# Expert rows weighed on ScalarE and summed on GpSimd, instead of both in one operation on VectorE

## The chip, the core and the metric

The kernel runs on one core of a Trainium2 chip. The metric is the device time of one execution in microseconds (us); lower is better. A core has five engines with a queue of instructions each: TensorE (PE, matrix products), VectorE (DVE), ScalarE (ACT), GpSimd (POOL) and SyncE (SP, which here only issues DMAs). Each runs its own queue in program order, and engines wait for each other on semaphores.

## The reference

One layer: `out = x + attention(xn) + experts(xn)`, with `xn` the layer norm of `x`. x has 16 x 512 rows of 128 floats.

```python
x = L0_attn_query
xn = _layernorm(x, axis=-1)
x = x + _L0_attn_ref(xn, ...) + _L0_ffn_ref(xn, Wg, W1, b1, W2, b2)
...
# _L0_ffn_ref: 8 experts, the two best of each row count
scores = x_flat @ Wg
topk_scores, topk_idx = jax.lax.top_k(scores, K)
topk_w = jax.nn.softmax(topk_scores, axis=-1)
cw = (jax.nn.one_hot(topk_idx, E, dtype=x.dtype) * topk_w[..., None]).sum(axis=1)
for e in range(E):
    h = jax.nn.gelu(x_flat @ W1[e] + b1[e], approximate=False)
    out_e = h @ W2[e] + b2[e]
    y = y + cw[:, e:e + 1] * out_e
```

The attention is over the 8 heads of each row, not over rows: per row complex states are built, turned by a few gates, multiplied head by head (the "pattern"), put through a softmax for four circuits and used to weigh the values (the "weighted" products). For the change it matters only that it fills the engines around the expert sum.

## The kernel before

The 8192 rows are 16 blocks of 512 (128 partitions x T = 4 x 128 floats). The program is a hand-written order: steps k = -1 to 16, and in each step every engine has its list of calls for block k, for the block before (o = k - 1) and for the one after (n = k + 1). Step 8 spans about 826 to 911 us of the profiled execution, step 9 to 1002, step 10 to 1103, step 14 about 1362 to 1438; step 16 is only the end.

**Experts.** Four blocks are a group. `route` and `row_numbers` (VectorE) find for each row its two experts, the gates and the places in a table that is sorted by expert; GpSimd scatters the rows of xn there (32 indirect DMAs a group, L1294), in the steps 2, 6 and 10 and the step behind each, as well as at the start for the first group. The table is worked off in 39 tiles a group, some ten tiles a step (TensorE `tile_up`, `tile_down`; ScalarE `gelu`, `copy_turn`). When a group is done, GpSimd gathers both results of each row back (`gather`, 8 indirect DMAs a block, into a tile of `got`; for the last two blocks into two unused buffers of xnT), and `combine` adds them to `yacc`, the output block that already holds x and the attention's part. Its step and place are set by `combined_at`: blocks 0, 4 and 8 in the middle of steps 4, 8 and 12; 1 and 2 in step 5, 5 and 6 in step 9, 9 and 10 in step 13, of which the first in the middle and the second at the end; 3, 7 and 11 in the middle of steps 6, 10 and 14; 12 in the middle and 13 and 14 at the end of step 15; 15 in step 16. SyncE stores a block at the start of the step after.

**What stands around it.** VectorE in the middle of a step: `pattern_power` (ends with `below`), `combine`, `turned_states` (L1720), `probabilities` (expo), `value_phase`, `grown_twice` (fxyT, L1705), then the weighted products w0 and w1 (L1665), the sum of w4 (L1689), and so on. ScalarE there: `turn`, `score_exp`, the squares of `control2` (L1036, L1037), `pass_last` (a DMA from its queue, after turned_states), one tile with gelu, the square root `amplitude` (L1085), on which all weighted products wait. GpSimd makes the products pattern 2 and 5 (L1268, 128x1024 each half) and w4, w5, w6 (L1276, four parts each) in one slot of `prod`, so each waits for VectorE's sum of the one before; and the sums of squares sqx (L1259), for which TensorE waits with `grow_once` and `grow_twice` (L786).

**End of a step.** VectorE: product w7, `combine` of the second block, sum of w7; then step k + 1: the product pattern 0, `route` if it is a routed step (2, 6, 10), the sum of w6, more sums, pattern 1, `row_numbers`, `clip_and_mix` (L1760). ScalarE: `abs_sign` (L1103, L1105), then `copy_sums` (L1072) in a routed step, `copy_tile` of kq (L1057), `copy_v`, gelu. The product w4 is `products(k, ("weighted", 4))` in the code, its sum `sums(k, ("weighted", 4))`.

Of the kernel before, what the change touches and what calls it, by code (L numbers as in the profile page):

```python
# [128 lines left out]
def build(nc, query, W_qkv, b_qkv, W_out, b_out, quantum_weights, photonic_phases, entanglement_gates,  # L129
# [28 lines left out]
    with ExitStack() as ctx:  # L158
# [256 lines left out]
        added_step = signal("added_step", 2 * T)  # L415
# [15 lines left out]
        def exists(k):  # L431
            return 0 <= k < NB
# [512 lines left out]
        def _(act):  # L945
# [191 lines left out]

            def copy_mT(k):
                act.wait_ge(mT_psum.sem, mT_psum.value(k))
                if k >= 1:  # L1140
                    act.wait_ge(o_psum.sem, o_psum.value(k - 1))
                act.activation(measT[:], ps_t[:], ACT.Copy).then_inc(mT_ready.sem, 1)
# [17 lines left out]
            for k in STEPS:  # L1160
# [42 lines left out]
                if exists(n):  # L1203
                    pass_last(n)
                tiles(k, 5, 6)
# [18 lines left out]
                if exists(k):  # L1224
                    abs_sign(k, 2)

        @block.gpsimd
        def _(pool):
# [84 lines left out]

            def scatter_part(k, part):
# [9 lines left out]
            for k in STEPS:  # L1324
# [15 lines left out]
                if exists(k):  # L1340
                    products(k, ("weighted", 4))
                    products(k, ("weighted", 5))
# [4 lines left out]
                for b in gathered_at.get(k, [])[3:]:  # L1347
                    gather(b)

        @block.vector  # L1350
        def _(dve):
# [425 lines left out]
            def combine(k):  # L1777
                g, at = k // GROUP, combine_order.index(k)
                dve.wait_ge(got_landed.of(at), got_landed.value(at))
                dve.wait_ge(gates_step.sem, gates_step.value(g))  # L1780
                dve.wait_ge(attn_added.sem, attn_added.value(k))
                for choice in range(2):
                    for t in range(T):
                        if choice == 1:
                            dve.wait_ge(added_step.sem, added_step.value(at, t + 1))
                        tile = k % GROUP * T + t
                        dve.scalar_tensor_tensor(yacc[:, k % YS, t, :], got_at(at)[:, choice, t, :],
                                                 gates[:, g % GS, choice, tile:tile + 1], yacc[:, k % YS, t, :],
                                                 ALU.mult, ALU.add).then_inc(added_step.sem, 1)

# [8 lines left out]
            for k in STEPS:  # L1799
# [49 lines left out]
                for b in combined_at.get(k, [])[0:1]:  # L1849
                    combine(b)  # L1850
# [28 lines left out]
                for b in combined_at.get(k, [])[1:]:  # L1879
                    combine(b)  # L1880
# [27 lines left out]
```

## Time and profile before

| | |
|---|---|
| time of three runs | 1533.66 us median (1532.86 to 1537.47) |
| the profiled execution's own time | 1530.29 us |
| its span, first to last instruction | 1528.3 us |
| instructions | 19285 |
| mean granted TensorE clock | 0.873 of full speed |
| HBM read, written | 113.95 MB, 32.14 MB |

The profile shows one execution: when each engine was busy, with which line, and what ended each wait. The chain that ended last is followed back from the last instruction, at each step to what released it; only what stands on it sets the time. Most of it is a braid of all engines that repeats in each step (about 85 us a step).

### The profile page before, as it was taken

The numbers are of one execution on the slowest core, as the hardware profiler recorded it, in microseconds if no ns is written. First come the engines' busy times: TensorE is split into PE (matmuls) and PEld (weight loads), VectorE is DVE, ScalarE is ACT, GpSimd is POOL, SyncE is SP. The second block draws the span as 40 slices with busy tenths as digits, with TensorE's granted clock in tenths as the row PEclk, the third lists the DMA queues.
The fourth block names the chain that finished last, engine by engine and source line by source line (L and its number), as shares of the span: only waits on it lengthen the run. The fifth ranks groups of instructions, "written<-read, shape, count | busy, mean of one in ns | idle before, by whom it ended". The sixth has DMA issues, their size and how long they took to land.

```text
span 1528.3 us, 19285 instructions
## 1 busy us (share of the span) xinstructions
PE 1109.9 (73%) x5921; PEld 849.3 (56%) x5921; DVE 1269.2 (83%) x1546; ACT 792.0 (52%) x1610; POOL 765.0 (50%) x596
## 2 busy tenths in 40 slices
PE   4355696869788796866969696883977878586834
PEld 2324474747566574745747474672755657374623
DVE  4653899898997997879978979797789898799976
ACT  3424475664647474554646556373545657365321
POOL 2073424365645355375455444657614544554673
PEclk9987897989999898878979798897989989798866
DMA  7333242332415152331524233152331516242111
GB/s 213 97 100 93 54 135 59 117 105 67 145 48 170 39 156 70 107 118 53 152 66 130 76 108 103 51 166 64 111 87 56 146 38 180 56 123 79 40 41 35
DMA packets 111558, 147.37 MB, mean 96 GB/s; under 512 B 15777, under 2 KB 85089, under 8 KB 110945
## 3 DMA queue, kind: packets, MB, share of 16 engines
q1 hardware_dynamic: 102240, 125.15, 27.3%
q0 software_dynamic: 8192, 16.79, 3.4%
q10 hardware_dynamic: 1024, 4.20, 2.1%
q8 instruction: 49, 0.80, 0.2%
q14 instruction: 53, 0.43, 0.1%
HBM read 113.95 MB, written 32.14 MB: 96 GB/s over the span
## 4 chain that ended last, share of the span: by engine, by line
PE 48%; issue 13%; DVE 12%; POOL 12%; ACT 11%; DMA 1%; SPq 1%; ACTq 0%; DVEq 0%; POOLq 0%
PE ps_r L786 8%; PE ps_t L739 7%; PE ps_h L660 7%; PE ps_q L739 5%; PE ps_f L668 5%; PE ps_t L746 4%; POOL sqx L1259 3%; PE ps_k L726 3%; POOL rows_in L1294 3%; POOL prod L1268 3%; POOL got L1309 2%; DVE pat L1689 2%; ACT hid L1122 2%; POOL prod L1276 2%; DVE xy L1481 1%
## 5 line engine op out<-in xcount | busy, mean ns | idle before, releaser
L786 PE MATMUL ps_r<-sqx,mats 128*128 128x512 f32 x256 | 182.9, 853 | 199.5 <-POOL sqx L1259 181.1
L1276 POOL TENSOR_TENSOR prod<-expo,vT 128x512 f32<-128x512 f32 x192 | 236.9, 1266 | 137.6 <-DVE u L1689 97.7
L1268 POOL TENSOR_TENSOR prod<-kq 128x1024 f32<-128x1024 f32 x64 | 149.9, 2364 | 283.1 <-ACT kq L1057 283.0
L1122 ACT ACTIVATE hid<-ps_h,w_tile 128x128 f32<-128x128 f32 x624 | 178.5, 371 | 138.0 <-PE ps_h L660 132.1
L1689 DVE TENSOR_REDUCE pat<-prod 128x128 f32<-128x2048 f32 x96 | 217.1, 2275 | 0.6
L660 PEld LDWEIGHTS ps_h<-turned,w_tile 128*128 128x128 f32 x1248 | 172.5, 207 | 78.0 <-issue 54.2
L660 PE MATMUL ps_h<-turned,w_tile 128*128 128x128 f32 x1248 | 180.9, 292 | 37.8 <-issue 18.8
L786 PEld LDWEIGHTS ps_r<-sqx,mats 128*128 128x128 f32 x256 | 59.4, 257 | 267.3 <-POOL sqx L1259 187.2
L1259 POOL TENSOR_TENSOR sqx<-sqx,sqy 128x512 f32<-128x512 f32 x64 | 87.0, 1380 | 226.3 <-ACT sqy L1037 160.6
L1665 DVE TENSOR_TENSOR prod<-expo,ps_v 128x2048 f32<-128x2048 f32 x80 | 180.8, 2279 | 8.9 <-PE ps_t L739 5.9
L1660 DVE TENSOR_TENSOR prod<-ps_q,kq 128x1024 f32<-128x1024 f32 x128 | 150.3, 1215 | 36.4 <-PE ps_q L842 19.1
L1689 DVE TENSOR_REDUCE u<-prod 128x256 f32<-128x2048 f32 x64 | 145.9, 2281 | 39.0 <-POOL prod L1276 38.5
L668 PE MATMUL ps_f<-w_tile,hid 128*128 128x128 f32 x1248 | 170.9, 282 | 0.5 <-ACT turned L1115 0.5
L1294 POOL DMA_INDIRECT rows_in<-xn,row_of x128 | 138.4, 1081 | 49.1 <-issue 35.4
L668 PEld LDWEIGHTS ps_f<-w_tile,hid 128*128 128x128 f32 x1248 | 158.2, 199 | 0.8 <-ACT hid L1122 0.6
L1309 POOL DMA_INDIRECT got<-rows_out,row_of x112 | 128.6, 1148 | 32.2 <-issue 29.9
L739 PE MATMUL ps_q<-prod,ident 128*128 128x256 f32 x512 | 118.0, 390 | 19.5 <-DVE prod L1665 19.5
L739 PE MATMUL ps_t<-prod,ident 128*128 128x256 f32 x512 | 125.7, 402 | 6.1 <-DVE prod L1665 3.2
L739 PEld LDWEIGHTS ps_q<-prod,ident 128*128 128x128 f32 x512 | 100.7, 197 | 41.8 <-DVE prod L1665 22.2
L739 PEld LDWEIGHTS ps_t<-prod,ident 128*128 128x128 f32 x512 | 101.1, 203 | 21.7 <-issue 3.8
L1103 ACT ACTIVATE u_sgn<-ps_q,tiny 128x512 f32<-128x512 f32 x16 | 11.0, 687 | 181.7 <-PE ps_q L739 181.7
L746 PE MATMUL ps_t<-u,sup_mats 128*128 128x512 f32 x128 | 65.6, 659 | 20.4 <-DVE u L1481 20.3
(265 smaller groups left out, 2075.0 us busy)
## 6 DMA issues: line engine op xcount, KB each, us to landing
w_tile<-w_cat SPq DMA_DIRECT2D x156, 514.0 KB
x_tile<-rows_in SPq DMA_DIRECT2D x156, 64.0 KB
rows_out<-turned SPq DMA_DIRECT2D x156, 64.0 KB
rows_in<-u SPq DMA_DIRECT2D x2, 2496.0 KB, 11.9
yacc<-in_L_attn_query_dram SPq DMA_DIRECT2D x16, 256.0 KB, 4.3
out_dram<-yacc SPq DMA_DIRECT2D x16, 256.0 KB, 3.2
x_sb<-in_L_attn_query_dram SPq DMA_DIRECT2D x11, 256.0 KB, 4.3
b_tile<-b_parts SPq DMA_DIRECT2D x156, 0.8 KB
```

Source lines behind the costliest of these rows:

```text
L660: last = nc.tensor.matmul(ps_h[:, c, :], w_tile[:, n % WS, c * P:(c + 1) * P], turned[:, x_turn(n) % FS, 0, :], start=True, stop=True)
L668: nc.tensor.matmul(ps_f[:, 1, :], hid[:, n % 2, c, :], w_tile[:, n % WS, HID + c * C:HID + (c + 1) * C], start=(c == 0), stop=False)
L739: last = nc.tensor.matmul(ps_u[part][:, ABS_PARTS[part].index(unit[1]), :], ident[:], prod[:, slot, j * 256:(j + 1) * 256], start=(j == 0) ...
L786: nc.tensor.matmul(ps_r[:, bank, :], m, sqx[:, g, :], start=True, stop=True).then_inc(sig.sem, 1)
L1122: act.activation(hid[:, n % 2, c, :], ps_h[:, c, :], ACT.Gelu, bias=w_tile[:, n % WS, HID + HC * C + c:HID + HC * C + c + 1]).then_inc(hid ...
L1268: last = pool.tensor_tensor(set_of(2, part), q, other, ALU.mult)
L1276: last = pool.tensor_tensor(dst[:, at], w[:, at], v[:, at], ALU.mult)
L1294: pool.indirect_dma_start(out=rows_in[g % GI], out_offset=bass.IndirectOffsetOnAxis(ap=row_of[:, g % GS, choice, t:t + 1], axis=0), in_=xn ...
L1309: pool.indirect_dma_start(out=got_at(at)[:, choice, t, :], out_offset=None, in_=rows_out[g % GS], in_offset=bass.IndirectOffsetOnAxis(ap=r ...
L1660: last = dve.tensor_tensor(set_of(slot, part), q, other, ALU.mult)
L1665: last = dve.tensor_tensor(weighted_slot(slot, unit[1]), w, v, ALU.mult)
L1689: dve.tensor_reduce(dst, src, AX_X, ALU.add).then_inc(summed.sem, 1)
```

## The change

`combine` (16 blocks, on VectorE, eight operations `yacc = got * gate + yacc` of 128x128 each) goes. In its place ScalarE has `weigh_rows`: eight copies a block in place, `got = got * gate`, one for each choice and row tile. GpSimd has `add_rows`: two sums a block of 128x512, `yacc = yacc + got[choice]`. ScalarE's place is behind `pass_last` for the first block of a step and at the step's very end for the others; GpSimd's is between the products w4 and w5 for the first and at the step's end for the others. GpSimd waits for half a block (four copies) before each sum, and for its own first sum before the second.

```diff
--- before.py
+++ after.py
@@ -412,7 +412,8 @@
         turn_copied = signal("turn_copied")
         hidden_psum = signal("hidden_psum")
         hidden_ready = signal("hidden_ready", HC)
-        added_step = signal("added_step", 2 * T)
+        added_step = signal("added_step", 2)
+        rows_weighed = signal("rows_weighed", 2 * T)
 
         block = ctx.enter_context(nc.Block())
 
@@ -1135,6 +1136,16 @@
                         gelu(n + 1)
                     copy_turn(y_turn(n), slice(0 if s + 2 < TILES else 1, 2))
 
+            def weigh_rows(k):
+                g, at = k // GROUP, combine_order.index(k)
+                act.wait_ge(got_landed.of(at), got_landed.value(at))
+                act.wait_ge(gates_step.sem, gates_step.value(g))
+                for choice in range(2):
+                    for t in range(T):
+                        tile = k % GROUP * T + t
+                        act.activation(got_at(at)[:, choice, t, :], got_at(at)[:, choice, t, :], ACT.Copy,
+                                       scale=gates[:, g % GS, choice, tile:tile + 1]).then_inc(rows_weighed.sem, 1)
+
             def copy_mT(k):
                 act.wait_ge(mT_psum.sem, mT_psum.value(k))
                 if k >= 1:
@@ -1202,6 +1213,8 @@
                     control2(n)
                 if exists(n):
                     pass_last(n)
+                for b in combined_at.get(k, [])[0:1]:
+                    weigh_rows(b)
                 tiles(k, 5, 6)
                 if exists(k):
                     amplitude(k)
@@ -1223,6 +1236,8 @@
                 tiles(k, 9, None)
                 if exists(k):
                     abs_sign(k, 2)
+                for b in combined_at.get(k, [])[1:]:
+                    weigh_rows(b)
 
         @block.gpsimd
         def _(pool):
@@ -1311,6 +1326,15 @@
                             in_offset=bass.IndirectOffsetOnAxis(ap=row_of[:, g % GS, choice, k % GROUP * T + t:k % GROUP * T + t + 1],
                                                                 axis=0)).then_inc(got_landed.of(at), 16)
 
+            def add_rows(k):
+                at = combine_order.index(k)
+                pool.wait_ge(attn_added.sem, attn_added.value(k))
+                for choice in range(2):
+                    pool.wait_ge(rows_weighed.sem, rows_weighed.value(at, (choice + 1) * T))
+                    if choice == 1:
+                        pool.wait_ge(added_step.sem, added_step.value(at, 1))
+                    tt(yacc[:, k % YS], yacc[:, k % YS], got_at(at)[:, choice], ALU.add, added_step)
+
             def scatter_part(k, part):
 
                 for g, at in ((routed_group(k), part), (routed_group(k - 1) if k >= 0 else None, 4 + part)):
@@ -1339,6 +1363,9 @@
                     gather(b)
                 if exists(k):
                     products(k, ("weighted", 4))
+                for b in combined_at.get(k, [])[0:1]:
+                    add_rows(b)
+                if exists(k):
                     products(k, ("weighted", 5))
                 scatter_part(k, 2)
                 scatter_part(k, 3)
@@ -1346,6 +1373,8 @@
                     products(k, ("weighted", 6))
                 for b in gathered_at.get(k, [])[3:]:
                     gather(b)
+                for b in combined_at.get(k, [])[1:]:
+                    add_rows(b)
 
         @block.vector
         def _(dve):
@@ -1774,20 +1803,6 @@
                 dve.wait_ge(base_loaded.of(k), base_loaded.value(k))
                 tt(yacc[:, k % YS], ps_t[:].rearrange("p (t c) -> p t c", t=T), yacc[:, k % YS], ALU.add, attn_added)
 
-            def combine(k):
-                g, at = k // GROUP, combine_order.index(k)
-                dve.wait_ge(got_landed.of(at), got_landed.value(at))
-                dve.wait_ge(gates_step.sem, gates_step.value(g))
-                dve.wait_ge(attn_added.sem, attn_added.value(k))
-                for choice in range(2):
-                    for t in range(T):
-                        if choice == 1:
-                            dve.wait_ge(added_step.sem, added_step.value(at, t + 1))
-                        tile = k % GROUP * T + t
-                        dve.scalar_tensor_tensor(yacc[:, k % YS, t, :], got_at(at)[:, choice, t, :],
-                                                 gates[:, g % GS, choice, tile:tile + 1], yacc[:, k % YS, t, :],
-                                                 ALU.mult, ALU.add).then_inc(added_step.sem, 1)
-
             first_norms()
             angle_constants()
             normalise(0)
@@ -1846,8 +1861,6 @@
                     grown_once(n, 1)
                 if exists(k):
                     pattern_power(k)
-                for b in combined_at.get(k, [])[0:1]:
-                    combine(b)
                 if exists(n):
                     turned_states(n)
                 if routed is not None:
@@ -1876,8 +1889,6 @@
                     sums(k, ("weighted", 5))
                 if exists(k):
                     products(k, ("weighted", 7))
-                for b in combined_at.get(k, [])[1:]:
-                    combine(b)
                 if exists(k):
                     sums(k, ("weighted", 7))
```

ScalarE, the end of step 9 and the start of step 10 (routed). Before (u_sgn and u are `abs_sign`, tile_sums is `copy_sums`, kq `copy_tile`, hid `gelu`):

```order
L1122 ACTIVATE hid<-ps_h,w_tile 128x128 x4
L1115 ACTIVATE turned<-ps_f 128x256
L1103 ACTIVATE u_sgn<-u,tiny 128x512
L1105 ACTIVATE u<-u 128x512
L1072 ACTIVATE tile_sums<-ps_t 128x128
L1057 ACTIVATE kq<-ps_k 128x512
L1063 ACTIVATE ps_v<-vT 128x512
L1122 ACTIVATE hid<-ps_h,w_tile 128x128 x4
L1115 ACTIVATE turned<-ps_f 128x256
L1103 ACTIVATE u_sgn<-u,tiny 128x512
```

And in the changed kernel:

```order
L1123 ACTIVATE hid<-ps_h,w_tile 128x128 x4
L1116 ACTIVATE turned<-ps_f 128x256
L1104 ACTIVATE u_sgn<-u,tiny 128x512
L1106 ACTIVATE u<-u 128x512
L1146 ACTIVATE got<-got,gates 128x128 x8
L1073 ACTIVATE tile_sums<-ps_t 128x128
L1058 ACTIVATE kq<-ps_k 128x512
L1064 ACTIVATE ps_v<-vT 128x512
L1123 ACTIVATE hid<-ps_h,w_tile 128x128 x4
L1116 ACTIVATE turned<-ps_f 128x256
```

Eight copies in place (got, by gates) now stand between `abs_sign` and `copy_sums`; what follows is as before.

GpSimd, from the second part of step 9 (gathers of block 6, then w4, w5, w6 as prod<-expo,vT) to the first products of step 10 (prod<-kq is a pattern product, rows_in the scatter). Before:

```order
L1309 DMA got<-rows_out,row_of 128x128 x8
L1276 TENSOR_TENSOR prod<-expo,vT 128x512 x12
L1268 TENSOR_TENSOR prod<-kq 128x1024 x2
L1294 DMA rows_in<-xn,row_of 4992x128 x10
L1309 DMA got<-rows_out,row_of 128x128 x8
L1268 TENSOR_TENSOR prod<-kq 128x1024 x2
L1259 TENSOR_TENSOR sqx<-sqx,sqy 128x512 x2
```

And in the changed kernel:

```order
L1324 DMA got<-rows_out,row_of 128x128 x8
L1291 TENSOR_TENSOR prod<-expo,vT 128x512 x4
L1274 TENSOR_TENSOR yacc<-yacc,got 128x512 x2
L1291 TENSOR_TENSOR prod<-expo,vT 128x512 x8
L1274 TENSOR_TENSOR yacc<-yacc,got 128x512 x2
L1283 TENSOR_TENSOR prod<-kq 128x1024 x2
L1309 DMA rows_in<-xn,row_of 4992x128 x10
L1324 DMA got<-rows_out,row_of 128x128 x8
L1283 TENSOR_TENSOR prod<-kq 128x1024 x2
L1274 TENSOR_TENSOR sqx<-sqx,sqy 128x512 x2
```

The twelve parts of w4 to w6 are now cut after the first four by the two sums of block 5, and the two sums of block 6 stand ahead of the pattern product and the scatters.

ScalarE, the last instructions of the program (steps 15 and 16; measT is `copy_mT`). Before:

```order
L1103 ACTIVATE u_sgn<-ps_t,tiny 128x512
L1105 ACTIVATE u<-ps_t 128x512
L1103 ACTIVATE u_sgn<-u,tiny 128x512
L1105 ACTIVATE u<-u 128x512
L1103 ACTIVATE u_sgn<-u,tiny 128x512
L1105 ACTIVATE u<-u 128x512
L1142 ACTIVATE measT<-ps_t 128x512
```

And in the changed kernel:

```order
L1104 ACTIVATE u_sgn<-ps_t,tiny 128x512
L1106 ACTIVATE u<-ps_t 128x512
L1104 ACTIVATE u_sgn<-u,tiny 128x512
L1106 ACTIVATE u<-u 128x512
L1146 ACTIVATE got<-got,gates 128x128 x8
L1146 ACTIVATE xnT<-xnT,gates 128x128 x8
L1104 ACTIVATE u_sgn<-u,tiny 128x512
L1106 ACTIVATE u<-u 128x512
L1153 ACTIVATE measT<-ps_t 128x512
L1146 ACTIVATE xnT<-xnT,gates 128x128 x8
```

Sixteen copies (blocks 13 and 14) now stand ahead of the last sign and absolute value, and eight (block 15) behind measT.

## Rows read from the trace of the kernel before

**Rows 1.** The page's first part: busy us (share of the span) xinstructions.

```profile
PE 1109.9 (73%) x5921; PEld 849.3 (56%) x5921; DVE 1269.2 (83%) x1546; ACT 792.0 (52%) x1610; POOL 765.0 (50%) x596
```

**Rows 2.** Groups of VectorE: line, operation, shapes, count | busy us, mean ns | idle before.

```profile
L1787 DVE SCALAR_TENSOR_TENSOR yacc<-got,gates,yacc 128x128 f32<-128x128 f32 x112 | 34.9, 381 | 0.0
```

**Rows 3.** The chain in order of time: start us, us, what.

```profile
691.97 1.23 DVE yacc L1787 x5
...
1052.92 1.23 DVE yacc L1787 x5
```

**Rows 4.** Timeline of ScalarE, step 8: start us, us, instructions [idle before <-releaser].

```profile
851.79 1.25 ACT L991 ACTIVATE xn<-x_sb,moments,rstd 128x128 f32<-128x128 f32 x3
...
866.88 1.04 ACT L1037 ACTIVATE sqy<-xy 128x1024 f32<-128x1024 f32 x1
...
868.96 1.28 ACT L1122 ACT_TABLE_LOAD   x1 [1.03 <-DVE fxyT L1720]
870.25 1.14 ACT L1122 ACTIVATE hid<-ps_h,w_tile 128x128 f32<-128x128 f32 x4
...
872.98 1.15 ACT L1085 ACTIVATE expo<-expo,eps_amp 128x1024 f32<-128x1024 f32 x1
```

**Rows 5.** GpSimd's sums of squares: ns min/median/max, first and last start.

```profile
L1259 POOL TENSOR_TENSOR sqx<-sqx,sqy x64: 1253/1265/2251, 75.1 to 1405.8; 128x512 f32<-128x512 f32 x64
```

**Rows 6.** Timelines of VectorE, TensorE and GpSimd, middle of step 8.

```profile
874.48 4.47 DVE L1665 TENSOR_TENSOR prod<-expo,ps_v 128x2048 f32<-128x2048 f32 x2
...
877.87 7.07 PE L739 MATMUL ps_q<-prod,ident 128*128 128x256 f32 x32
...
881.60 4.94 POOL L1276 TENSOR_TENSOR prod<-expo,vT 128x512 f32<-128x512 f32 x4 [2.40 <-DVE u L1689]
```

**Rows 7.** Timelines of ScalarE and TensorE, middle of step 6.

```profile
702.33 1.15 ACT L1085 ACTIVATE expo<-expo,eps_amp 128x1024 f32<-128x1024 f32 x1 [1.14 <-DVE expo L1481]
...
706.30 2.53 PE L786 MATMUL ps_r<-sqx,mats 128*128 128x512 f32 x4 [3.07 <-DVE fxyT L1705]
```

**Rows 8.** Timelines of ScalarE, VectorE and GpSimd, start of step 10.

```profile
1001.68 0.26 ACT L1072 ACTIVATE tile_sums<-ps_t 128x128 f32<-128x128 f32 x1
...
1004.91 2.34 DVE L1660 TENSOR_TENSOR prod<-ps_q,kq 128x1024 f32<-128x1024 f32 x2
1007.36 0.17 DVE L1629 TENSOR_SCALAR scan<-scan 128x8 f32<-128x8 f32 x1
...
1002.57 4.67 POOL L1268 TENSOR_TENSOR prod<-kq 128x1024 f32<-128x1024 f32 x2 [14.41 <-ACT kq L1057]
1011.60 1.76 POOL L1294 DMA_INDIRECT rows_in<-xn,row_of  x1 [4.36 <-DVE tile_expert L1649]
```

**Rows 9.** Timelines of VectorE and GpSimd, start of step 6.

```profile
644.70 1.45 DVE L1535 TENSOR_SCALAR ss<-ss 128x96 f32<-128x96 f32 x1
...
643.73 4.68 POOL L1268 TENSOR_TENSOR prod<-kq 128x1024 f32<-128x1024 f32 x2 [17.14 <-ACT kq L1057]
```

**Rows 10.** Timelines of VectorE and ScalarE, end of step 13 and start of 14.

```profile
1347.35 4.12 DVE L1787 SCALAR_TENSOR_TENSOR yacc<-got,gates,yacc 128x128 f32<-128x128 f32 x8
...
1362.41 2.36 DVE L1660 TENSOR_TENSOR prod<-ps_q,kq 128x1024 f32<-128x1024 f32 x2
...
1361.70 0.58 ACT L1057 ACTIVATE kq<-ps_k 128x512 f32<-128x512 f32 x1
```

**Rows 11.** Timelines of VectorE and ScalarE, end of step 15 and step 16.

```profile
1498.95 3.16 DVE L1787 SCALAR_TENSOR_TENSOR yacc<-got,gates,yacc 128x128 f32<-128x128 f32 x8
1502.04 2.17 DVE L1787 SCALAR_TENSOR_TENSOR yacc<-xnT,gates,yacc 128x128 f32<-128x128 f32 x8
...
1523.29 2.19 DVE L1787 SCALAR_TENSOR_TENSOR yacc<-xnT,gates,yacc 128x128 f32<-128x128 f32 x8
...
1502.20 0.63 ACT L1105 ACTIVATE u<-u 128x512 f32<-128x512 f32 x1
1508.63 0.72 ACT L1103 ACTIVATE u_sgn<-u,tiny 128x512 f32<-128x512 f32 x1 [5.80 <-DVE u L1689]
...
1520.22 0.60 ACT L1142 ACTIVATE measT<-ps_t 128x512 f32<-128x512 f32 x1 [10.21 <-PE ps_t L754]
```

## The prediction

> **What bounds the kernel now.** The page's first part comes first: VectorE is busy 83% of the span and TensorE 73% [rows 1]. No engine is full, so moving work off the fullest one is worth only what the chain that ended last holds of it. The groups of VectorE give the size of what goes: 112 of the 128 operations of `combine` cost 34.9 us [rows 2], 16 more about 5.5 by a like length. Reported lengths overlap, though: eight of them pass in 2.2 us. Then I asked the chain where `combine` stands on it. It does in the middle of steps 6 and 10 [rows 3] and at the end of the program; in the other steps the chain runs past it, through TensorE, GpSimd or ScalarE. So of some 35 us of VectorE time about 11 are on the path: twice 2.1, then 5.1 and 2.2 [rows 11].
>
> **The costs of the new work.** No row shows a 128x128 ScalarE copy from SBUF with a scale per partition. The nearest from below is gelu with one pointer operand, four in 1.14 us, so one each 0.26 us and eight in 2.2; from above the layer norm with two pointers, three in 1.25 us, so one each 0.39 and eight in 3.2 [rows 4]. Copy has one pointer, but reads SBUF; I take 0.29 each, 2.35 for a block. It needs no table load (`copy_tile` and the squares stand beside others without one). A GpSimd sum of 128x512 stands in the trace: 1.25 us at least, 1.27 in the middle, 2.25 at worst [rows 5]; two are 2.55 us. The Trainium skill ("GPSIMD Engine Reference", section 3.1) states that a two-input fp32 operation is about half as fast there as on VectorE. An estimate from its 4497 ns for 2048 elements is 1.12 us for 512, so 2.25 for two; by it the end would cost 0.3 us less than below. The trace has the same form at 1.27, and the sum uses that row.
>
> **Steps 4, 8 and 12, middle: 0.** The place is ahead of gelu and of the square root `amplitude`, on which w0, w1 (VectorE) and w4 (GpSimd) wait. Before, ScalarE's squares ended at 867.9 and it stood 1.03 us, because `pass_last` waited for `turned_states`, which was behind `combine` [rows 4]. That wait goes with the 2.1 us of `combine`. So eight copies fill 1.1 us of standing and push the square root by 2.35 - 1.1 = 1.2 us, to an end at 875.3 instead of 874.1. VectorE starts w0 at 875.4 instead of 874.48 and ends it at 877.65; TensorE took it up at 877.87 [rows 6], so it still comes in time. VectorE's saved 2.1 us turn into waiting for the root. The sums on GpSimd go between w4 and w5, where it stood 2.40 us for VectorE's sum of w4 [rows 6]; they take 2.55, so w5 is late by a few tenths beyond the 1.2, and its reader on VectorE comes 2 us after it. Price nothing, with 0.3 us to spare; if the cover is gone, up to 1 us a step. In steps 5, 9 and 13 w4 has eight gathers ahead of it in GpSimd's queue and the root is ready long before: nothing too.
>
> **Steps 6 and 10, middle: -2.3 and -2.8.** Here the root waited for VectorE (1.14 us) and TensorE waited 3.07 us for `grown_twice`, which is behind `combine` [rows 7]. The root stays where it was in step 6 (1.1 earlier by the wait, 1.1 by pass_last, 2.35 later by the copies) and comes 0.9 earlier in step 10, still before VectorE needs it. VectorE reaches `grown_twice` some 2.1 us sooner, a little more where its small gate operations no longer run beside GpSimd's sums. -5.1 in all.
>
> **Start of steps 6 and 10: +2.9 each.** The second block of steps 5, 9 and 13 is weighed at the end of the step, and that puts eight copies ahead of `copy_sums` (1001.68), `copy_tile` and the next gelu on ScalarE, which works nearly without a gap there. TensorE's ranking waits for tile_sums: +2.35, and with it `q_operands`. VectorE's pattern product, before at 1004.91 [rows 8], now starts with q at about 1005.5, although VectorE is 1.0 us ahead of its old time by then; the rest of its gain is lost waiting for the first q. On GpSimd the sums go ahead of the pattern product: first half weighed at 1003.0, sums until 1005.6, product 1005.6 to 1010.3 instead of 1002.57 to 1007.24 [rows 8]. Now the lock. `row_numbers` began its SBUF operations at 1007.36, just behind that product. Where a small VectorE operation did meet such a product it took 1.45 us instead of 0.21, until the product's first half was over [rows 9]. Moved to 1007.9 it meets the second half, waits until 1010.3, and ends at 1014.2 instead of 1011.3. The scatters wait for it [rows 8], and from there GpSimd runs without a gap up to the sums that TensorE waits for. 2 x 2.9 = +5.8. Behind this the Trainium skill ("SBUF — State Buffer", section "SBUF: two separate sides") says that the port pair shared by VectorE and GpSimd is held for a whole instruction and the other engine fully blocks; the trace agrees at [rows 9], and without that rule the start would cost 0.6 a step and the sum come out 4.6 lower.
>
> **Start and middle of step 14: +2.4, +0.5.** Here `combine` took 4.12 us on VectorE, since it met GpSimd's w6 [rows 10]. The gain is again lost: the pattern product needs kq, whose copy slips from 1361.70 to 1364.05 [rows 10], so it starts at 1364.7, not 1362.41. The clip behind it meets GpSimd's product, which the sums have pushed to 1365.6 to 1370.3; clip and multiply end 3.2 us late. TensorE's and ScalarE's slack takes 0.8 of that before the next squares. In the middle of step 14 the 1.2 us of the root stay: VectorE has no wait until the next step's kq, where 0.7 is absorbed.
>
> **End: -0.9.** Both blocks 13 and 14 leave VectorE, 5.1 us ahead of the last two sums; ScalarE waited for them until 1508.63 [rows 11]. But now 16 copies stand ahead of that abs and sign: 1502.7 + 16 x 0.29 = 1507.4, a gain of 1.2, not 5.1. Block 15 is weighed behind measT (1520.22), done with the last attention sum; then two GpSimd sums replace 2.19 us of VectorE [rows 11] by 2.55: +0.3.
>
> **Queues.** SyncE waits for the sums before it stores, and behind that wait are the loads of x, of the base block and of the weights. At the start of steps 6, 10 and 14 the store of the second block now waits until about 1005.6, 15 us later than before, but the weights' own wait for TensorE (1007 by then) is later, so nothing. The gathers' wait for `added_step` is now on GpSimd's own earlier work, two blocks back.
>
> **Sum:** -5.1 + 5.8 + 2.9 - 0.9 = +2.7 us on the profiled execution's 1530.3. The median of the runs shown, 1533.66, is 3.4 above that; on its scale 1536.
>
> **The rivals.**
> 1. *Faster: VectorE's time comes back.* If the copies and sums are all covered, the 11.5 us of `combine` on the chain go and 2.55 us of sums come at the end: -9, 1525. For it: the chain's rows. Against: at the starts and at the end ScalarE stands between VectorE's gain and its use. Chance 0.18.
> 2. *Slower: the copies run at the layer norm's 0.39.* Eight then take 3.2: the end +1.5 and +0.8, three starts +0.85 each, the middles of 4, 8, 12 and 14 about +0.5 each once 0.3 of slack is gone: +7, 1543. It decides from about 0.33 a copy; GpSimd sums nearer 2.25 than 1.27 would do the same through w5. Chance 0.3.
> 3. *No lock at `row_numbers`.* VectorE slips between two GpSimd instructions: 4.6 less, 1532, still within 0.3% of 1533.66. Chance 0.12.
>
> My forecast, a trade of nearly equal parts, has 0.4, with 1531 to 1541 as its own range. The range 1527 to 1545 takes in the slower rival and about half of the first. 0.3% is 4.6 us and about what a measurement of this kernel tells from no change: faster 0.2 (rival 1, a little of 3), slower 0.35 (rival 2, the upper part of the forecast), same 0.45.
>
> **What would show it.** VectorE busy falls by about 35 us and its waits grow as much, for expo L1085's root and for kq. ScalarE and GpSimd gain some 35 to 50 and 41 us. The scatters of steps 6 and 10 start about 3 us later after the step's first product, with stretched tiny VectorE operations in `row_numbers`. TensorE's wait before `grow_twice_more` in steps 6 and 10 falls from 3.07 to about 1. At the end the last sign of u starts straight behind the 16 copies. I am wrong if a copy takes 0.26 or 0.39 each, if `row_numbers` isn't stretched, or if the starts of steps 6, 10 and 14 aren't late.

## The result, and the profile after

Twenty executions of each kernel, side by side: the changed kernel takes 1539.01 us (median; 1536.01 to 1542.20), the one before 1534.01 (1528.55 to 1538.37). The ratio is 1.0034, with a 95% interval of 1.0024 to 1.0045, which is +5.2 us (3.7 to 6.9): slower, by just over the 0.3% that was called the limit of what can be told. The prediction had +2.7 us and 1536, with 1527 to 1545 as the range; "no change" had the largest chance (0.45), "slower" 0.35. The profiled execution took 1540.28 us with a span of 1538.5. In all comparisons two slow executions are left out, one of the kernel before (1580.43 us) and one of the kernel with nine middle blocks moved (3600.07 us).

The first part of the page of the changed kernel, to set beside [rows 1]:

```profile
PE 1124.6 (73%) x5921; PEld 855.6 (56%) x5921; DVE 1238.5 (80%) x1418; ACT 828.4 (54%) x1738; POOL 811.5 (53%) x628
```

VectorE lost 31 us of work and 128 instructions; ScalarE gained 36 us and GpSimd 47, and the time went up. `combine` had been 39.3 us of VectorE (34.9 in [rows 2] and 4.4 for the blocks in xnT); some 8 us came back in operations that now take longer, most of it in the multiply by rz (`expo<-expo,rz`, 29.0 us in 16 instead of 23.8), which took 1.98 us beside GpSimd's sum in step 8 and 1.28 clear of it before. The new work itself, as groups (line, operation, shapes, count | busy us, mean ns | idle before and what ended it):

```profile
L1274 POOL TENSOR_TENSOR yacc<-yacc,got 128x512 f32<-128x512 f32 x28 | 35.5, 1269 | 47.4 <-ACT got L1146 45.4
L1146 ACT ACTIVATE got<-got,gates 128x128 f32<-128x128 f32 x112 | 34.0, 386 | 0.0
```

A copy is reported with 386 ns, but the reports overlap: eight stand in 2.43 us below, so each one takes (2.43 - 0.39) / 7 = 0.29 us. That is the value chosen between 0.26 and 0.39. The sums take 1.27 us each, as [rows 5] had it. So both prices of the new work were right, and the rival with copies at 0.39 falls. GpSimd's sums waited 45.4 us for the copies, in three places; these are the starts of steps 6, 10 and 14.

The start of step 10, timelines of ScalarE, GpSimd and VectorE, to set beside [rows 8]:

```profile
1005.29 2.43 ACT L1146 ACTIVATE got<-got,gates 128x128 f32<-128x128 f32 x8
1007.62 0.25 ACT L1073 ACTIVATE tile_sums<-ps_t 128x128 f32<-128x128 f32 x1
1007.78 0.58 ACT L1058 ACTIVATE kq<-ps_k 128x512 f32<-128x512 f32 x1
...
1006.69 2.68 POOL L1274 TENSOR_TENSOR yacc<-yacc,got 128x512 f32<-128x512 f32 x2 [15.21 <-ACT got L1146]
1009.33 4.64 POOL L1283 TENSOR_TENSOR prod<-kq 128x1024 f32<-128x1024 f32 x2
...
1009.60 2.36 DVE L1689 TENSOR_TENSOR prod<-ps_q,kq 128x1024 f32<-128x1024 f32 x2 [1.58 <-PE ps_q L843]
1011.88 0.16 DVE L1657 TENSOR_SCALAR scan<-ps_t 128x8 f32<-128x8 f32 x1
1012.07 1.94 DVE L1658 TENSOR_SCALAR scan<-scan 128x8 f32<-128x8 f32 x1
```

Here the mechanism of the forecast stands in one view. The copies push tile_sums and kq; the sums push GpSimd's product to 1009.33 to 1013.97; and the second small operation of `row_numbers`, 0.17 us before, starts at 1012.07 and ends at 1014.01, with that product. The one before it reads PSUM (ps_t) and is not held.

The middle of step 6, ScalarE, VectorE and TensorE, beside [rows 7]:

```profile
709.96 1.15 ACT L1086 ACTIVATE expo<-expo,eps_amp 128x1024 f32<-128x1024 f32 x1
...
711.20 4.48 DVE L1694 TENSOR_TENSOR prod<-expo,ps_v 128x2048 f32<-128x2048 f32 x2 [2.01 <-ACT expo L1086]
...
713.54 2.64 PE L740 MATMUL ps_q<-prod,ident 128*128 128x256 f32 x11 [0.61 <-DVE prod L1694]
```

TensorE no longer waits 3.07 us for `grown_twice`. But now VectorE stands 2.01 us for the square root, which stands behind the copies. This wait is new in nearly every step: in the view of waits, VectorE's w0 waited 1.6 us in two places before, and after:

```profile
DVE prod L1694 <- ACT expo L1086: 17.9, 11, 2.0
```

### The profile page after: what moved, and what is told of

It reads as the page before. It is cut to its first block and busy times, and to the rows that moved or that the text cites. A ratio compares the mean times of both kernels' runs of the same rounds, so it can differ in the third digit from the quotient of the medians.

```text
span 1538.5 us, 19349 instructions
## 1 busy us (share of the span) xinstructions
PE 1124.6 (73%) x5921; PEld 855.6 (56%) x5921; DVE 1238.5 (80%) x1418; ACT 828.4 (54%) x1738; POOL 811.5 (53%) x628
## 5 line engine op out<-in xcount | busy, mean ns | idle before, releaser
L661 PE MATMUL ps_h<-turned,w_tile 128*128 128x128 f32 x1248 | 185.9, 297 | 39.3 <-issue 19.0
L1274 POOL TENSOR_TENSOR sqx<-sqx,sqy 128x512 f32<-128x512 f32 x64 | 94.3, 1495 | 226.7 <-ACT sqy L1038 163.2
L669 PE MATMUL ps_f<-w_tile,hid 128*128 128x128 f32 x1248 | 175.7, 287 | 0.5 <-ACT turned L1116 0.5
L669 PEld LDWEIGHTS ps_f<-w_tile,hid 128*128 128x128 f32 x1248 | 162.9, 204 | 0.8 <-ACT hid L1123 0.6
L1116 ACT ACTIVATE turned<-ps_f 128x256 f32<-128x256 f32 (+1 forms) x164 | 62.7, 383 | 35.4 <-PE ps_f L653 24.5
```

The costliest lines, as they stand in the source:

```text
L661: last = nc.tensor.matmul(ps_h[:, c, :], w_tile[:, n % WS, c * P:(c + 1) * P], turned[:, x_turn(n) % FS, 0, :], start=True, stop=True)
L669: nc.tensor.matmul(ps_f[:, 1, :], hid[:, n % 2, c, :], w_tile[:, n % WS, HID + c * C:HID + (c + 1) * C], start=(c == 0), stop=False)
```

## The experiments

Each kernel was timed against the one before in five rounds, 6 to 12 executions of each. The interval in brackets is at 95%; 0.001 of the ratio is 1.5 us. Those that move only some blocks share this edit: for blocks in `MOVED` ScalarE and GpSimd work as in the changed kernel, for the others `combine` stays at its old place on VectorE, with a semaphore for each of the two.

```diff
+    MOVED = [...]
...
                 for b in combined_at.get(k, [])[0:1]:
-                    weigh_rows(b)
+                    if b in MOVED:
+                        weigh_rows(b)
```

### The last block back on VectorE: `MOVED` is all but 15

> The changed kernel, but block 15 (the last one of the program) is combined on VectorE as before; the other 15 blocks stay on ScalarE and GpSimd. Theory A (a late GpSimd makes the end of the program long): after the last sum 5.5 us pass to the end of the span when GpSimd made it, 2.8 when VectorE did, so this run ends 2.7 + 0.4 = 3.1 us earlier than the changed kernel, about +1.9 us against before. Theory B (my forecast's term): only the difference of the sums, 0.3 to 0.4 us; then about +4.7 us against before.

Measured: 1.0021 (1.0004 to 1.0037), +3.2 us (0.6 to 5.7). That is 2.0 less than the changed kernel's +5.2, but the interval takes in both theories. The traces settle it together with the next run.

### The kernel before, with GpSimd last

```diff
+            pool.wait_ge(added_step.sem, added_step.value(NB - 1))
+            pool.tensor_tensor(sqx[:, 0], sqx[:, 0], sqy[:, 0], ALU.add)
```

> The kernel before, with one more GpSimd sum of 128x512 (into a buffer that nobody reads) that waits for the last sum of block 15 on VectorE. It ends 1.3 us behind that sum, and the end of the span was 2.8 us behind it. Theory A (the end waits long behind GpSimd's last instruction when that comes late, some 5.5 us): about +4 us against before. Theory B (only the store counts): 0.

Measured: 1.0041 (1.0027 to 1.0056), +6.3 us for one instruction of 1.3 us that nobody waits for. First its trace: GpSimd's timeline, and SyncE's waits from 1522 on (engine, line, waited for: us in total, times, longest):

```profile
1530.42 1.26 POOL L1350 TENSOR_TENSOR sqx<-sqx,sqy 128x512 f32<-128x512 f32 x1 [17.13 <-DVE yacc L1789]
...
SPq L158 <- PEq L158: 4.2, 1, 4.2
SPq L627 <- DMA out_dram<-yacc: 1.8, 1, 1.8
```

The same two views of the changed kernel:

```profile
1530.31 2.66 POOL L1274 TENSOR_TENSOR yacc<-yacc,xnT 128x512 f32<-128x512 f32 x2 [3.71 <-DVE yacc L1510]
...
SPq L158 <- PEq L158: 2.9, 1, 2.9
```

And of the kernel before:

```profile
SPq L158 <- PEq L158: 0.2, 1, 0.2
```

L158 is the end of the program, where the engines meet. GpSimd's last instruction ended at 1531.68 with the span at 1537.2, and at 1532.97 with the span at 1538.5: 5.5 us both times. Before, VectorE's last sum ended at 1525.48 and the span at 1528.3, which is 2.8, the time of the store. In the run with block 15 on VectorE it is again 2.8. So it is GpSimd that makes the end long when it finishes last, by 2.7 us, and the sums themselves add 0.4. The trace does not show what GpSimd does in these 5.5 us. Of this run's +6.3 the end explains 4.0 (6.9 us from VectorE's last sum to the end of the span, instead of 2.8), which is just below its interval (4.1 to 8.6); where the rest comes from is open.

### Only the blocks in the middle of a step: 0, 1, 3, 4, 5, 7, 8, 9, 11

> Only the blocks that are combined in the middle of a step are moved to ScalarE and GpSimd (0, 1, 3, 4, 5, 7, 8, 9, 11); blocks 2, 6, 10 and 12 to 15 stay on VectorE. Theory A (my forecast's terms: -2.3 in step 6, -2.8 in step 10, +0.5 in step 14, nothing in 4, 5, 8, 9, 12, 13): -4.6 us against before. Rival (the sums delay the product w5 and the square root comes late in each of the steps 4, 5, 8, 9, 12 and 13, as the +1.5 us a step seen in steps 4 and 5 of the one profile could mean): -4.6 + 6 x 0.7, so about 0.

Measured: 0.9982 (0.9970 to 0.9994), -2.8 us (-4.6 to -0.9): between the two, and nearer to Theory A. It was then split.

### Only 3 and 7

> Only blocks 3 and 7 (middle of steps 6 and 10) are moved to ScalarE and GpSimd, all others stay on VectorE. My forecast's terms -2.3 and -2.8: -5 us against before. Rival (the nine blocks of the middle gave -2.8 because the gain in steps 6 and 10 is itself smaller than forecast, not because steps 4, 5, 8, 9, 12, 13 and 14 cost something): -2 to -3 us.

Measured: 0.9969 (0.9948 to 0.9990), -4.8 us (-8.0 to -1.5). By the time alone the rival's -2 to -3 isn't excluded; the traces decide. In this run the middles of steps 6 and 10 take 14.93 and 14.87 us, where kernels with the blocks on VectorE take 17.2 to 18.6. The forecast's two gains hold.

### Only 0, 4, 8, 1, 5, 9

> Only blocks 0, 4, 8 and 1, 5, 9 are moved (middle of steps 4, 8, 12 and 5, 9, 13); all others stay on VectorE. My forecast: 0 against before, since the square root is 1.2 us later, but TensorE takes up w0 as before, and w5's reader has 2 us to spare. Rival (what is missing between -4.8 us of blocks 3 and 7 and -2.8 us of all nine blocks of the middle is lost here, about 0.3 us a block, and 0.5 in step 14): +1.5 us.

Measured: 1.0024 (1.0012 to 1.0036), +3.7 us. The forecast of nothing falls, and the rival's +1.5 is too small as well. (With -4.8 for blocks 3 and 7 this leaves -1.1, where all nine middles gave -2.8; the intervals allow both.) What it costs and when can be read in a view of windows: length, then busy us and count of TensorE's matmuls, its weight loads, VectorE, ScalarE and GpSimd, then TensorE's granted clock as a share of full speed, the DMA share and GB/s. The middles of steps 8 and 9, in the kernel before:

```profile
863.00:878.00 15.00, 8.50 (x27) 5.29 (x28) 14.79 (x25) 10.03 (x16) 6.40 (x6) 0.66 0.23 61
948.00:963.00 15.00, 8.73 (x27) 5.52 (x28) 14.79 (x25) 9.81 (x15) 8.55 (x8) 0.66 0.30 78
```

In the kernel before with GpSimd last, whose middle steps are the same program:

```profile
865.00:879.00 14.00, 7.47 (x27) 4.26 (x28) 13.79 (x25) 10.05 (x16) 5.37 (x5) 0.76 0.28 73
948.00:963.00 15.00, 7.17 (x25) 4.33 (x26) 14.73 (x28) 11.35 (x17) 7.31 (x7) 0.77 0.26 67
```

And in the changed kernel:

```profile
866.00:881.00 15.00, 7.91 (x27) 4.12 (x28) 12.78 (x17) 12.29 (x23) 5.97 (x5) 0.77 0.32 85
951.00:966.00 15.00, 7.83 (x27) 3.96 (x27) 12.83 (x18) 12.44 (x24) 8.28 (x7) 0.77 0.35 93
```

From the start of rowmax in `pattern_power` to TensorE's first matmul of w0, the middle of step 8 took 14.91 us in the execution from which the forecast was made. In the kernel with GpSimd last it took 13.85. With the block moved it takes 14.93: the square root behind the copies sets it. In the six middles of the four kernels that move these blocks it is 14.92 or 14.93 us in 19 of 24, and 15.0 to 15.2 in the other five. The mean clock is 0.66 in the first two windows and 0.76 or 0.77 in the other four.

What made TensorE take w0 up late, and so was to hide the copies, is eight matmuls of the experts (ps_h) ahead of w0. TensorE's timeline in step 8, before and with GpSimd last, and in step 12 before:

```profile
873.08 1.88 PE L660 MATMUL ps_h<-turned,w_tile 128*128 128x128 f32 x8
...
874.78 1.05 PE L660 MATMUL ps_h<-turned,w_tile 128*128 128x128 f32 x8
...
1238.53 1.77 PE L660 MATMUL ps_h<-turned,w_tile 128*128 128x128 f32 x8
```

The granted clock over just these was 0.54, 1.00 and 0.58 of full speed, that is, mostly the lower level (1.2 GHz), all at the upper one (2.4 GHz), and mostly the lower. In the 60 such middles with the block on VectorE (six in each of ten executions) the eight matmuls take 1.05 to 1.92 us, and the middle follows them: 13.85 to 13.93 us where they take 1.05, 14.2 to 14.3 at 1.13 to 1.26, 14.8 to 14.9 at 1.8, 14.9 to 15.2 at 1.9. The mean clock of the whole window is a poor guide to it: step 12 before has 0.77 and still takes 14.80 us. One execution had been read for the forecast, and in it five of the six middles (all but step 13, 14.35 us) had the slow matmuls.

### Only the blocks at the end of a step: 2, 6, 10

> Only the blocks combined at the end of steps 5, 9 and 13 are moved (2, 6, 10); all others stay on VectorE. Theory A (my forecast): the starts of steps 6 and 10 get 2.9 us later each, that of 14 by 2.4 us, so +8.2 us against before; in the trace the second small operation of row_numbers takes about 2 us instead of 0.17. Rival (the shift of the starts is slack that the next steps give back): +2 to +4 us.

Measured: 1.0039 (1.0026 to 1.0053), +6.0 us (4.0 to 8.1), between the two expectations. The stretched operation of the forecast is there (1.71 and 1.75 us at the starts of steps 6 and 10); the price is three quarters of the forecast's.

### The same three, without the sums

```diff
-                for choice in range(2):
-                    pool.wait_ge(rows_weighed.sem, rows_weighed.value(m, (choice + 1) * T))
...
-                    tt(yacc[:, k % YS], yacc[:, k % YS], got_at(at)[:, choice], ALU.add, added_pool)
+                pool.wait_ge(rows_weighed.sem, rows_weighed.value(m, 2 * T))
+                pool.memset(sink[:], 0.0).then_inc(added_pool.sem, 2)
```

> As the run in which blocks 2, 6 and 10 alone are moved and weighed at the end of the step, but GpSimd's two sums for these three blocks are left out (a memset of two columns stands in their place, so the experts' part is missing from these blocks' output). What is left is the eight copies ahead of copy_sums and copy_tile and the 2.1 us that VectorE saves. Theory A (the sums' share is that they push GpSimd's pattern product about 1 us further, which locks row_numbers and the clip of step 14 longer, and hold up the store): about 3 us less than that run's +6, so +3 us against before. Rival (the copies ahead of kq and tile_sums are the whole loss): still about +6 us.

Measured: 1.0024 (1.0012 to 1.0037), +3.7 us. That is 2.3 below the run with the sums, near the 3 expected, but the two intervals overlap. In the trace the stretched operation of step 6 is down to 0.73 us from 1.71, since GpSimd's product starts with kq (647.00) and ends sooner. So by the medians the sums carry some third of the loss and the copies ahead of kq and tile_sums the rest; how it is shared is not told apart by these two times.

### The same three, weighed earlier

```diff
+                for b in combined_at.get(k, [])[1:]:
+                    if b in MOVED:
+                        weigh_rows(b)
                 tiles(k, 8, 9)
...
                     abs_sign(k, 2)
-                for b in combined_at.get(k, [])[1:]:
-                    if b in MOVED:
-                        weigh_rows(b)
```

> Blocks 2, 6 and 10 moved as in the run of the second blocks, but ScalarE weighs them one tile before the end of the step, ahead of the tile at which it stood 3.6 us for TensorE, so that the copies end before abs_sign and the sums fall into GpSimd's 14 us gap ahead of the pattern product. Theory A (the +6 us of these blocks is all from the copies ahead of copy_sums and copy_tile and from the sums ahead of the pattern product): the loss goes, 0 to -1 us against before; copy_sums and kq start as before, and row_numbers has no stretched operation. Rival (the loss comes from moving the work at all: later stores, GpSimd's sums beside VectorE's work): +3 to +6 us.

Measured: 0.9995 (0.9980 to 1.0010), -0.8 us. The whole loss of +6.0 is gone, by a move of the same eight copies within ScalarE's queue. (The expectation says one tile; in the trace the copies stand ahead of the last three tiles of step 5 and the last two of steps 9 and 13, and ahead of two calls of `abs_sign`.) With the copies the sums and the store come earlier too. GpSimd's timeline ahead of step 10: the sums are done before kq comes.

```profile
994.71 2.68 POOL L1292 TENSOR_TENSOR yacc<-yacc,got 128x512 f32<-128x512 f32 x2 [4.81 <-ACT got L1162]
1003.91 4.65 POOL L1301 TENSOR_TENSOR prod<-kq 128x1024 f32<-128x1024 f32 x2 [6.52 <-ACT kq L1073]
```

### Weighed early, but summed in the middle of `row_numbers`

```diff
                     products(k, ("pattern", 2))
+                for b in combined_at.get(o, [])[1:]:
+                    if b in MOVED:
+                        add_rows(b)
```

> As the run with blocks 2, 6 and 10 weighed early, but GpSimd's two sums of each stand behind its pattern product of the next step, where VectorE is in row_numbers; the copies are out of the way and kq is on time. Theory A (small VectorE operations and GpSimd's sums lock each other out): row_numbers and the cast behind it end 2.3 to 2.6 us later in steps 6 and 10, and clip and multiply in step 14 about 1 to 2 us, so +5 to +7 us against the run with early sums; the stretched operations stand out in the trace. Rival (the lock costs next to nothing, the copies were the whole loss): 0 to +1 us against that run.

Measured: 1.0092 (1.0069 to 1.0115), +14.1 us, twice what was expected. Step 6 shows the lock. GpSimd's sums, and VectorE's first operations that read SBUF (0.17 us each in [rows 8]):

```profile
648.10 2.67 POOL L1292 TENSOR_TENSOR yacc<-yacc,got 128x512 f32<-128x512 f32 x2
...
646.56 1.60 DVE L1679 TENSOR_SCALAR scan<-scan 128x8 f32<-128x8 f32 x1
648.20 1.20 DVE L1680 TENSOR_SCALAR scan<-scan 128x8 f32<-128x8 f32 x1
649.43 0.17 DVE L1681 TENSOR_TENSOR scan<-scan 128x8 f32<-128x8 f32 x1
649.63 1.16 DVE L1682 TENSOR_TENSOR scan<-scan 128x8 f32<-128x8 f32 x1
```

The product's second half and each of the two sums hold up one small operation until they end; L1681 starts just as one sum has ended and passes in 0.17. Together +3.5 us here and +2.0 in step 10. The Trainium skill ("SBUF — State Buffer", section "SBUF: two separate sides") describes just this, a port pair held for a whole instruction; the trace agrees, with 0.17 against 1.2 to 1.6 us. But most of the loss is elsewhere: between w0 of step 13 and `pattern_power` of step 14 this kernel takes 84.0 us, and the kernels without late work 73.0 to 75.0. SyncE's timeline and TensorE's longest wait there:

```profile
1364.59 11.19 SPq L551 DMA_DIRECT2D out_dram<-yacc  x2
1375.82 0.51 SPq L543 DMA_DIRECT2D yacc<-in_L_attn_query_dram  x1
1377.56 0.36 SPq L562 DMA_DIRECT2D w_tile<-w_cat  x1
...
PE ps_h L676 <- issue: 12.1, 1, 12.1
```

The sums (stretched to 5.54 us by clip and multiply) end at 1375.4, the store waits for them, and the next load of expert weights stands behind the store: issued at 1377.56, against 1366.06 in the kernel before, of which this one is 2.8 us behind at w0 of step 13. TensorE stands 12.1 us for it. This is the queue that the forecast priced at nothing. In the changed kernel that was nearly so: its load is issued at 1372.01 with all of VectorE's and ScalarE's work 5.1 us late, and TensorE stands 3.1 us instead of 2.2.

### Blocks 13 and 14 (`LATE`) behind the last clip, all on VectorE

```diff
                 if exists(o):
                     clip_and_mix(o)
+                for b in combined_at.get(o, [])[1:]:
+                    if b in LATE:
+                        combine(b)
```

> The kernel before, all on VectorE, with only blocks 13 and 14 combined behind the last clip_and_mix instead of ahead of the last two sums of step 15. VectorE stood 5.2 us there for TensorE. Theory A (5.1 us of the chain's end): the last signs of u start 5.1 us earlier behind their sums, but not earlier than the products' PE work allows: -5 us against before. Rival (the wait moves to something else ahead of the last signs, TensorE's transposes of the last product): -1 to -3 us.

Measured: 0.9961 (0.9947 to 0.9975), -6.0 us (-8.1 to -3.8). VectorE's and ScalarE's timelines:

```profile
1502.71 4.48 DVE L1739 TENSOR_REDUCE u<-prod 128x256 f32<-128x2048 f32 x2
...
1512.11 2.18 DVE L1837 SCALAR_TENSOR_TENSOR yacc<-got,gates,yacc 128x128 f32<-128x128 f32 x8
1514.21 2.18 DVE L1837 SCALAR_TENSOR_TENSOR yacc<-xnT,gates,yacc 128x128 f32<-128x128 f32 x8
...
1507.23 0.72 ACT L1119 ACTIVATE u_sgn<-u,tiny 128x512 f32<-128x512 f32 x1 [0.74 <-DVE u L1739]
```

The two sums of u come straight behind the last product, and the expert rows are added while TensorE mixes. From w0 of step 15 to TensorE's last mix it is 31.46 us instead of 36.60: the whole 5.1.

### Together

> The two edits that gained by themselves, together: blocks 3 and 7 on ScalarE and GpSimd in the middle of steps 6 and 10, blocks 13 and 14 on VectorE behind the last clip, all else as before. Theory A (the gains stand at different places of the chain and add): -4.8 - 5.9 = -10 to -11 us against before. Rival (part of each was given by the same slack): -6 to -8 us.

Measured: 0.9936 (0.9905 to 0.9968), -9.8 us (-14.6 to -4.9; ten executions). The interval takes in the rival too. The trace has both gains in full: the middles of steps 6 and 10 take 14.93 and 14.88 us, and from w0 of step 15 to the last mix it is 31.44.

> As the combination of blocks 3 and 7 moved and 13 and 14 behind the clip, and besides blocks 2, 6 and 10 moved with the early weighing. Theory A (the early weighing is worth what it showed alone, -0.8 us and not told from nothing): -11 to -12 us against before, equal to the combination within 1 us. Rival (with VectorE less loaded at steps 5, 9 and 13, the weighed blocks only add load to GpSimd, whose sums meet VectorE's work): 1 to 3 us worse than the combination.

Measured: 0.9924 (0.9898 to 0.9949), -11.7 us (-15.6 to -7.8; six executions). The two are not told apart. Both beat the kernel before, and so the changed one: 1521.66 and 1521.53 us beside 1533.94.

## Why the prediction came out as it did

The landmarks of the timelines of all profiled executions give each stretch of the sum a mean. "Middle" is from rowmax of `pattern_power` to TensorE's first matmul of w0; "start" from that matmul to the next rowmax. Kept means that the blocks there stay on VectorE or, for the starts, are weighed early; the run with the sums in `row_numbers` is left out of the starts, and so is the one without sums.

| stretch | forecast, us | kept: mean (executions) | moved: mean (executions) | difference |
|---|---|---|---|---|
| middle of step 6 | -2.3 | 17.55 (8) | 15.00 (6) | -2.5 |
| middle of step 10 | -2.8 | 17.85 (8) | 14.91 (6) | -2.9 |
| middles of 4, 5, 8, 9, 12, 13 | 0 | 14.29 to 14.75 (10) | 14.93 to 15.08 (4) | +2.9 in all |
| middle of step 14 | +0.5 | 14.55 (11) | 14.92 (3) | +0.4 |
| start of step 6 | +2.9 | 90.28 (9) | 93.39 (3) | +3.1 |
| start of step 10 | +2.9 | 91.30 (9) | 92.72 (3) | +1.4 |
| start of step 14 | +2.4 | 74.08 (9) | 76.89 (3) | +2.8 |
| w0 of step 15 to the last mix | -1.2 | 36.60 | 35.71, 35.36 | -0.9, -1.2 |
| last `add_out` to the span's end | +0.3 | 5.15 | 8.27 | +3.1 |

The last column adds up to +7.3, above the timed +5.2 (3.7 to 6.9); the starts rest on three executions that differ by up to 4 us, and there the surplus may well be, but that isn't shown.

- **Middles of 6 and 10, and of 14: right**, in place and in size. One detail was not: the root does not come before VectorE needs it. TensorE's wait for `grown_twice` is gone altogether, and the root, for which VectorE stands 2.01 us in step 6, now sets the 14.9 us.
- **"Steps 4, 8 and 12, middle: 0" and the sentence on 5, 9 and 13: wrong.** The working ("the square root 1.2 us later, TensorE still takes w0 up in time") held for the execution it was read from. Its cover was eight matmuls at a low granted clock (1.9 us instead of 1.05). Without that the middle with the block on VectorE is 13.9 to 14.3 us, and with it moved the root makes it 14.9. In steps 5, 9 and 13 the root was not ready long before either: in step 9, with the nine middle blocks moved, it ends at 959.62 and w0 starts at 959.71. Six middles cost +2.9 by the traces and +3.7 (1.8 to 5.5) by the timed run.
- **Starts of 6, 10 and 14: late as foretold, but the lock was overpriced.** Weighing earlier takes the loss from +6.0 to -0.8, so copies and sums at the end of a step are its cause. But over the executions of the table the start of step 6 is +1.8 us late at VectorE's pattern product (forecast +0.6) and +1.4 in `row_numbers` behind it (forecast +2.3). In step 10 `row_numbers` is 1.6 longer, while the pattern product comes 0.8 earlier than in the kept executions, and 0.6 is lost behind the clip. The reason is a small operation ahead of the pattern product, ss of 128x96. In the execution that was read it met only the end of the first half of GpSimd's product in step 10 (0.33 us instead of 0.21; w0 of step 9 to the clip in step 10: 48.34 us). In the other eight kept executions (50.1 to 50.6 us) it was held in each, and took 1.9 to 2.4 us. So the lock mostly changes its victim. All stretches of ss and the small scans together are 1.5 and 2.1 us in steps 6 and 10 with the blocks moved, and 1.1 and 1.6 us with them kept: the lock adds about 0.4 us a step, not 2.3.
- **End: the gain of 1.2 right.** In the changed kernel the last sign starts straight behind the sixteen copies, as foretold. **The last step, "+0.3", missed 2.7 us**: no row of the kernel before had GpSimd finish last.
- **Queues: right for this kernel by little.** With sums some 5 us later, the store would have held up the weights for 12 us.
- The rivals: the faster one failed as its own "against" said, at the starts and the end. The slower one (+9.5 on the kernel before, 1543) is further from the measured +5.2 than the forecast, and not its mechanism either: a copy takes 0.29, and what was missing came from the middles and from GpSimd's end. The third (no lock) is refuted as a mechanism by the stretched operation; as a price it was nearer than the forecast's 2.3 a step.

The collision that the change did not bring, in the kernel before with GpSimd last, VectorE's and GpSimd's timelines at the start of step 10:

```profile
1006.02 1.89 DVE L1537 TENSOR_SCALAR ss<-ss 128x96 f32<-128x96 f32 x1
...
1003.18 4.66 POOL L1268 TENSOR_TENSOR prod<-kq 128x1024 f32<-128x1024 f32 x2 [13.40 <-ACT kq L1057]
```

The same operation took 0.33 us when the forecast was made. The change moves the collision from it to `row_numbers`.

In sum: the two costs that were priced at nothing or nearly so are +2.9 and +2.7, and the start of step 10 takes 1.5 back. With the forecast's +2.7 that makes 6.8, above the timed +5.2 and just inside its interval. That the sum came so near is in part luck: two costs were missed, and a lock that the kernel before mostly paid already made up for some of it.

## What to carry to other kernels

A cover that hides an edit has to be looked up in more than one execution: if it comes from TensorE at a lower granted clock, it may be gone in the next one, and so may a collision between two engines come or go. A profile of the same program with a trivial edit is a cheap second sample. Where moved work stands in its engine's queue was worth more than which engine does it: the same eight copies of a block, with the sums behind them, cost +6.0 us at the end of a step and nothing two or three tiles earlier, and the last two blocks gained 6.0 us by going behind the last clip without leaving VectorE. Look where the engine that has the work stands idle next, before giving it to another one, and move only the blocks that the chain runs through.

## What the runs showed of the hardware

- The program's end took 5.5 us from GpSimd's last instruction in both kernels where that came last (the changed one and the one before with GpSimd last), and 2.8 us from VectorE's last sum where GpSimd had long been done (the kernel before and the one with block 15 on VectorE). The cause inside GpSimd is open.
- An in-place ScalarE copy of 128x128 in SBUF with a scale per partition passes every 0.29 us and is reported with 386 ns (changed kernel, 112 copies).
- A VectorE TENSOR_SCALAR or TENSOR_TENSOR on SBUF alone, even of 128x8, stands until the GpSimd instruction that it meets has ended (up to 1.9 us instead of 0.17 at 128x8, up to 2.4 instead of 0.21 at 128x96). One whose input is in PSUM took 0.15 to 0.16 beside the same product. A TENSOR_REDUCE on SBUF alone was not held either: ss<-xy took 1.74 us beside GpSimd's product in step 10 of the kernel before, and 1.74 clear of it in step 14.
- TensorE's granted clock over the same eight matmuls of the same program differed between executions, from 0.54 to 1.00 (1.88 and 1.05 us, step 8), and moved the middle of the step by 1.1 us.
